# A new order for every engine's steps and a new layout of the PSUM banks in a four-layer graph network kernel

## The chip, the cores and the metric

The kernel runs on one core of one Trainium2 chip, in one launch. The metric is the device time in microseconds (us) of that core; lower is better. The core has TensorE (matrix products and transposes, into PSUM), VectorE, ScalarE and GpSimd, and SyncE, which here only issues transfers. In the profile's rows they are PE (PEld for its weight loads), DVE, ACT, POOL and SP. TensorE has a granted clock that the profile shows as a share of full speed: 1.00 is 2.4 GHz, 0.50 is 1.2 GHz.

## What is computed

The input x is 32 graphs of 512 nodes with 128 features in float32; one 512 x 512 adjacency matrix is shared by all. Four layers follow each other. Each adds to x what it computes from h = max(layernorm(x), 0):

```
layer 0: hW = h @ Wo; scores from two projections of hW, leaky 0.1, masked by adj, softmax over axis 1
         out = att @ hW + h @ Ws
layer 1: h1 = h @ Wp + bp; scores s_src + s_dst, leaky 0.2, masked, softmax, times adj, @ h1
         h_gat = relu(layernorm(...)); h_gin = (1 + eps) * h_gat + adj @ h_gat
         z = relu(layernorm(h_gin @ W1 + b1)); out = relu(z @ W2 + b2 + h_gat)
layer 2: Wh = h @ W; scores f1 + f2, leaky 0.2, masked, softmax, @ Wh, + bias, elu
layer 3: out = (A * I) @ (h @ W[0]) + (A * (1 - I)) @ (h @ W[1]) + bias
         A = softmax of edge weights that are placed by the rank of each edge in adj
x = x + out, after each layer
```

## The kernel before

**Tiling.** The 32 graphs are cut into 16 groups of two (G = 2). A group's x is one SBUF tile of 128 partitions by 1024 float32, eight blocks of 128 features. Six groups can be under way at a time (NS = 6 sets of buffers). Each group passes through 56 named steps (the list STEPS): for each the list gives the number of PSUM banks that it opens and the engines that take part. There is a 17th stream of nine steps (PREP, written as group 16 here, letter g in the strings), which makes layer 3's matrix A; layer 3 of the first groups waits for it.

**Order.** Nothing is scheduled at run time. Each engine walks a fixed list of (group, step) pairs, and waits on semaphores in its steps. The list is written as one string per engine, TURNS: the k-th letter is the group whose next step (of those in which this engine takes part) comes k-th. Steps of one group keep their order on an engine; only how the groups interleave is free. TensorE has 469 such steps, VectorE 471, ScalarE 403, GpSimd 160, SyncE 32 (loads and stores).

**Banks.** PSUM has eight banks of 128 x 512 float32. A second string, HOMES, has one digit for each bank that TensorE's steps open, in TensorE's order: the bank's number. A step that opens a bank waits until the last reader of what was in it before has freed it.

The lines that do this:

```
for e, turns in TURNS.items():
    todo = [(name for name, _, engines in steps if e in engines.split()) for steps in [STEPS] * GROUPS + [PREP]]
    order[e] = [(int(g, GROUPS + 1), next(todo[int(g, GROUPS + 1)])) for g in turns]
...
for g, name in order["pe"]:
    for n in range(tiles_of[name]):
        bank = int(next(home))
...
def open_tile(u, name, s, n=0):
    slot, k = u.tile(name, n)
    pe.wait_ge(taken[slot], k + 1)
```

**The steps that matter below.**
- *Normalisation* (four times per group, and gats1 and mlps1 in layer 1): stat0 to stat3, gats1, mlps1 are eight bn_stats on VectorE (line 1176) and then, on GpSimd, ten small steps on 128 x 8 tiles (lines 431 to 446, function rstd_of); then scale0 to scale3, gat1, mlpb1 are eight activations on ScalarE (line 450), and norm0 to norm3, mlpb1 are eight transposes on TensorE (line 704), which ScalarE copies to HT.
- *Layer 0*: coef0 (TensorE, line 687, wcols; VectorE, lines 1188 to 1196), cmax0 (TensorE, line 795; VectorE, lines 1201 to 1210; ScalarE exponentials, lines 969 and 970), coefp0 (GpSimd, four small steps, lines 1114 to 1117), coefb0 (TensorE, CS and adj_top; VectorE, lines 1222 to 1231), feat0 (TensorE, Wo), split0 (VectorE, lines 1237 and 1242, each twice; ScalarE copies HI and HIB, lines 975 and 982), low0 (VectorE LOW, line 1247; GpSimd LOWB, line 1122), agg0 (TensorE, maskT with HI and LOW), self0 (TensorE, with HIB, LOWB and Ws; VectorE adds).
- *Layer 1*: feat1, top1, weigh1, spread1, att1a and att1b (attention of the two graphs), collect1, gats1, gat1, gatl1, gin1, mlpa1, mlps1, mlpb1, mlpc1. *Layer 2*: feat2, sums2, top2, spread2, att2a, att2b, elu2a, elu2b, elu2. *Layer 3*: shift3, feat3, agg3.
- *PREP*: erow, eoffm, eedge, eat, ecover, evalue, emask, esoft (VectorE, lines 1431 to 1438, after ScalarE's exponentials) and eturn (TensorE transposes, line 893; ScalarE copies a_hi, line 1060; VectorE a_lo, line 1446).

The setup ahead of the ordered walk (loads, masks, weights) ends at about 24 us and is the same in both kernels.

Of the kernel before, what the change touches and what calls it, by code (L numbers as in the profile page):

```python
# [117 lines left out]
    ("eturn", 4, "pe act dve"),  # L118
]
TURNS = {  # L120
    "pe": ("gggg01011200201g100221313240030410041013314041252513132052025521243143232013031535040003100110104511"
           "4254251145540250245102132322124264262673667437762426373234343447333644768486465876858676738787535778"
           "348584588489559859659956a99a5a6a679a997969669569657a67a56767778a778a7b7b8a6b869baba6a78ab7b88978a8ba"
           "8cb8b8bbcd9bd9bdca8a8ccd9d899a9c9aa9ca9aa9edeadceacbcdeccbecdcd9edebd9b9edebedbeecbfcfbefbebffbbfcfd"
           "adafcfdfaffdcfcccfccedcddedcfdfededfbfdeeeebfeeffefeffbfcdfcdcedfefef"),
    "dve": ("g021gggg1010g02g001314010012113220503401401231340232210351034351221054524125433423001153500250012130"
            "0441105025145111452204303541262431252724626226676337644267376253743438334777464638436868857847687887"
            "3455637884984856579a895599956899a95a76655a99a996768a965a77a956a667b766787797abab86877aab6bbab7bbac89"
            "a788d8bab88bc88bd99cdba8accddc89b9c9aeca9adacd9aedd9eb9cac9cceedbedcedee9bb9dcecfeadeebacbfdfbbfffbb"
            "edfffbbdacfcfeffddccaefcccdfdfeccdfdeecdffdeedbefedfeeffbfefecffdcdefef"),  # L130
    "act": ("g02101g210g01334200410130240115053012102104150223113510322014323004100031125115442025502410325140521"
            "342135342226436472764346227233457343344468683667548758636775353868747545848796895587596a968a8665a979"
            "6996756a9566975797776a78a789b6b88667aba877b8aa79aa98bc8ab8ac9bd8bd9ba8ba8c8d9b9caa999adaaebecc9debdc"
            "c9cbecaddb9b9ceebdcbedefcbfcdbbeaeffcdcbdadfafdefdfccebfccfdcdefdfdecfefedffeebdefbefefffceddcfcdeef"
            "fef"),
    "pool": ("02110031402135420231350415420150310210214563274626237463784783586384547959a8969a657a5967a7b686b87b7a"
             "bc89da889cbdacaed9cde99ebcebfdbafcafefdcbdcfedfbefcedfcdefef"),
    "sp": "345020611728394a5b6c7d8e9fabcdef",
}
HOMES = ("0123456710234567102345671203645024502714365027127504127502741361436150274674361530263704204372047620"  # L140
         "4376204371506265043715423603165427031370137013701654270541653421670615342706156364270153615142703516"
         "5165421703267053267054105410326570413261357045740261357042613570426135710457263103142603142640231657"
         "1657164023042571642571264307127152756430127645301452376017604523601745021367450215036274150451045316"
         "2712716271627160475316205476231054762310765410765414072653721401640146537201420653714065371425306710"
         "6710642537061706170610760176017642534523476347652347652031476576457645642073156204062407316540731652"
         "4073152640731526430742615305310745236216216074536530652106352106743542354210674267410351032674032516"
         "0734516073451620762076345135135143541207635412075634120637541206375413270654506132702761302024502761"
         "4376052145421542145214376052176432174360536050356217407374560213745602145376021453760241537602415")


def bcast(ap, n):
# [14 lines left out]
def gnn_kernel(nc, x, adj, Wo_d, Ws_d, att0_d, Wp_d, bp_d, asrc_d, adst_d, gatg_d, gatb_d, eps_d, W1_d, b1_d,  # L166
# [12 lines left out]
    with ctx:  # L179
# [62 lines left out]
        tile_at, mat_at, mat_of = {}, {}, []  # L242
        opened, home = [0] * BANKS, iter(HOMES)
        for g, name in order["pe"]:
# [1277 lines left out]
```

How the kernel before makes its waits and increments, by code:

```python
            @block.sync  # L455
            def _(sp):
                for t in range(T):
                    sp.dma_start(adj_raw[:, t, :], adj[t * P:(t + 1) * P, :]).then_inc(adj_loaded, 16)
                for s in range(NS // 2):
                    for b in range(G):
                        sp.dma_start(X[s][:, b::G, :],
                                     x.rearrange("b (t p) f -> b p t f", p=P)[s * G + b]).then_inc(x_loaded[s], 16)
                for dst, src in REST:
                    sp.dma_start(dst, src).then_inc(loaded["rest"], 16)
                for s in taken:
                    sp.sem_inc(s, 1)
                for s in sig["stored"]:
                    sp.sem_inc(s, 16)
                sp.wait_ge(loaded["rest"], 16 * len(REST))
# [1 line left out]
            @block.gpsimd  # L472
# [3 lines left out]
                nc.gpsimd.memset(work1[:], 1.0).then_inc(made["pool"], 1)  # L476
                nc.gpsimd.memset(minus_half[:], -0.5).then_inc(made["pool"], 1)
                nc.gpsimd.memset(ones_r[:].bitcast(F32), 1.0).then_inc(made["pool"], 1)
                for zeros in (pick, bias_p, bias_1, bias_2):
                    nc.gpsimd.memset(zeros[:].bitcast(F32), 0.0).then_inc(made["pool"], 1)
                pool.wait_ge(made["pool"], 9)
                nc.gpsimd.affine_select(out=ident[:], in_=ident[:], compare_op=ALU.not_equal, fill=1.0, base=0,
                                        pattern=[[-1, P]], channel_multiplier=1).then_inc(made["pool"], 1)
```

## Time and profile before

| | before |
|---|---|
| median of 3 runs | 1011.76 us (1009.36 to 1011.84) |
| profiled execution, its own time | 1009.46 us |
| its span, first to last instruction | 1007.7 us |
| busy: TensorE, VectorE, ScalarE, GpSimd | 943.0, 866.1, 632.5, 566.6 us |
| TensorE's granted clock, mean | 0.979 |
| a load of a group's x, issue to landing | 3.5 us (median) |

How to read it: an engine's busy time is the union of its instructions' times; a wait shows as idle time in front of an instruction, with what ended it. A half clock shows not as idle time but as longer instructions. A view by windows gives busy time and the granted clock for each stretch, and the timeline merges equal instructions that follow each other into one row (x8 is eight of them).

### The profile page before, as it was taken

How to read it: one execution, taken by the hardware profiler on the slowest of the kernel's cores; microseconds unless marked ns; L12 is line 12 of the kernel's file. 1: busy time of each engine (PE TensorE's matmuls, PEld its weight loads, DVE VectorE, ACT ScalarE, POOL GpSimd, SP SyncE). 2: the span in 40 equal slices, each digit the busy share in tenths (PEclk: the TensorE clock that was granted, in tenths of full speed). 3: DMA queues.
4: the chain of work that ended last, by engine and by line, in shares of the span. 5: the costliest groups of instructions: out<-in, count | busy, mean ns of one | idle time of the engine just before them, and what ended most of it. 6: DMA issues, size and time to landing. Idle time of an engine off the chain costs nothing. (4 is left out here: it accounts for less than half of the span.)

```text
span 1007.7 us, 21096 instructions
## 1 busy us (share of the span) xinstructions
PE 943.0 (94%) x7355; PEld 901.4 (89%) x7355; DVE 866.1 (86%) x2526; ACT 632.5 (63%) x1655; POOL 566.6 (56%) x1171
## 2 busy tenths in 40 slices
PE   5879999999999989999989999999999999997998
PEld 4779998998988989998989999899999998997897
DVE  6879898899979999978989987789989887887973
ACT  3435746875777755676675756777458676666751
POOL 3416356655477662763748645736646475556750
PEclk9978999999999999999999999999999999999999
DMA  5011000000011010011000101100100100000012
GB/s 136 1 36 28 2 1 1 2 1 1 2 43 42 2 44 1 1 43 43 2 1 2 43 2 43 43 1 13 32 1 2 42 2 1 17 7 2 1 43 63
DMA packets 38069, 19.97 MB, mean 20 GB/s; under 512 B 3142, under 2 KB 37452, under 8 KB 37964
## 3 DMA queue, kind: packets, MB, share of 16 engines
q1 hardware_dynamic: 36080, 18.42, 6.6%
q8 instruction: 59, 0.97, 0.4%
q10 hardware_dynamic: 1884, 0.21, 0.2%
q14 instruction: 46, 0.38, 0.1%
HBM read 10.23 MB, written 8.39 MB: 18 GB/s over the span
## 5 line engine op out<-in xcount | busy, mean ns | idle before, releaser
L450 ACT ACTIVATE Y<-X,SM 128x128 f32<-128x128 f32 x512 | 204.3, 489 | 70.8 <-POOL SM L446 70.6
L687 PE MATMUL ps<-HE,PT 128*128 128x129 f32 x2048 | 240.2, 276 | 2.7 <-ACT HE L999 1.7
L687 PEld LDWEIGHTS ps<-HE,PT 128*128 128x128 f32 x2048 | 233.5, 192 | 4.1 <-ACT HE L999 1.9
L1311 DVE SCALAR_TENSOR_TENSOR PT<-ps,CE,maskT 128x512 f32<-128x512 f32 x256 | 173.0, 741 | 13.3 <-PE ps L811 13.0
L442 POOL TENSOR_TENSOR SM<-SM,minus_half 128x8 f32<-128x8 f32 x96 | 162.9, 1696 | 7.6
L431 POOL TENSOR_TENSOR SM<-ST 128x8 f32<-128x8 f32 x96 | 29.7, 310 | 230.8 <-DVE ST L1176 230.8
L687 PE MATMUL ps<-W,HT 128*128 128x128 f32 (+1 forms) x768 | 125.9, 312 | 0.0
L687 PEld LDWEIGHTS ps<-W,HT 128*128 128x128 f32 x768 | 116.4, 194 | 8.8
L1176 DVE BATCH_NORM_STATS2 ST<-X 128x6 f32<-128x128 f32 x512 | 104.7, 277 | 2.6 <-DMA X<-in_x_dram 1.0
L704 PE MATMUL ps<-ident,Y 128*128 128x128 f32 x640 | 86.3, 282 | 13.2 <-ACT Y L450 11.0
L704 PEld LDWEIGHTS ps<-ident,Y 128*128 128x128 f32 x640 | 74.5, 146 | 16.8 <-ACT Y L450 14.1
L959 ACT ACTIVATE HT<-ps 128x512 f32<-128x512 f32 x96 | 51.9, 593 | 37.1 <-PE ps L704 36.6
L687 PE MATMUL ps<-HI,a_hi 128*128 128x256 f32 x256 | 73.2, 286 | 0.0
L687 PE MATMUL ps<-HI,a_lo 128*128 128x256 f32 x256 | 72.0, 281 | 0.0
L687 PE MATMUL ps<-LOW,a_hi 128*128 128x256 f32 x256 | 72.0, 281 | 0.0
L999 ACT ACTIVATE HE<-ps,HE 128x128 f32<-128x128 f32 x256 | 68.9, 381 | 0.0
L450 ACT ACTIVATE HE<-Y,SM 128x128 f32<-128x128 f32 x128 | 51.0, 488 | 17.6 <-POOL SM L446 17.5
L687 PE MATMUL ps<-gin_hi,LOW 128*128 128x512 f32 x128 | 57.8, 451 | 0.0
L1176 DVE BATCH_NORM_STATS2 ST<-Y 128x6 f32<-128x128 f32 x256 | 51.8, 274 | 5.0 <-ACT Y L1028 4.6
L450 ACT ACTIVATE Y<-Y,SM 128x128 f32<-128x128 f32 x128 | 50.9, 485 | 8.1 <-POOL SM L446 8.0
L1122 POOL TENSOR_TENSOR LOWB<-HE,HIB 128x1024 fp32r<-128x1024 f32 x16 | 36.2, 2260 | 26.0 <-ACT HIB L982 26.0
L687 PE MATMUL ps<-gin_hi,HI 128*128 128x512 f32 x128 | 50.4, 394 | 0.0
(260 smaller groups left out, 2355.5 us busy)
## 6 DMA issues: line engine op xcount, KB each, us to landing
X<-in_x_dram SPq DMA_DIRECT2D x32, 256.0 KB, 3.5
out_dram<-X SPq DMA_DIRECT2D x32, 256.0 KB, 2.8
adj_raw<-in_adj_dram SPq DMA_DIRECT2D x4, 256.0 KB, 3.8
W<-in_L_gnn_W_dram SPq DMA_DIRECT2D x2, 64.0 KB, 3.8
W<-in_L_gnn_W_dram SPq DMA_DIRECT2D x1, 128.0 KB, 3.5
bias<-in_L_gnn_bias_dram SPq DMA_DIRECT2D x2, 64.0 KB, 3.9
Wo<-L_gnn_others_weight_dram ACTq DMA_DIRECT2D x1, 64.0 KB, 3.2
feat1w<-in_L_gnn_Wp_dram ACTq DMA_DIRECT2D x1, 64.0 KB, 3.6
```

The lines of the kernel that those rows point to most:

```text
L431: TT(sm[:, S_DIF, :], st[:, :, 1], st[:, :, 4], ALU.subtract)
L442: link(TT(sm[:, S_RSTD, :], sm[:, S_VAR, :], minus_half[:], ALU.pow))
L450: a = nc.scalar.activation(dst[:, n, 0:F], src[:, n, 0:F], func, scale=SM[s][:, S_RSTD, n:n + 1], bias=SM[s][:, S_SHIFT, n:n + 1])
L687: return nc.tensor.matmul(o, w, m, start=start, stop=stop, skip_group_check=True)
L704: mm = T_(o[:, t * P:(t + 1) * P], Y[s][:, t * G + b, 0:F], ident[:])
L959: a = A(HT[s][:, b, :], o, ACT.Relu)
L999: a = A(HE[s][:, k, 0:F], o[:, 2 * P * b:2 * P * b + F], ACT.Identity, scale=HE[s][:, k, F:F + 1])
L1122: TT(LOB[s], VA[s], HIB[:].bitcast(F32), ALU.subtract).then_inc(sig["by_pool"][s], 1)
L1176: a = V.bn_stats(ST[s][:, n, :], src(n))
L1311: a = V.scalar_tensor_tensor(out=PT[r][:, j, :], in0=o, scalar=CE[s][:, c:c + 1], in1=maskT[:, j, :].bitcast(F32), op0=ALU.max, op1=ALU.mult)
```

## The change

Only the strings TURNS and HOMES are new: no instruction is added, removed or resized. The new strings come from the same kind of planning as the old ones, with three costs changed in the plan: an instruction of VectorE and one of GpSimd in SBUF exclude each other, TensorE runs at half its clock for part of the time, and the banks are laid out again for the new order. On TensorE 335 of 469 steps stand at another place, by 1.6 places on average and 15 at most; on VectorE 360 of 471, by 1.9 and 16; on ScalarE 303 of 403, by 1.8 and 21; on GpSimd 88 of 160, by 0.8 and 4; on SyncE 7 of 32, by 3 at most.

The diff, cut to the first line of each string:

```diff
 TURNS = {
-    "pe": ("gggg01011200201g100221313240030410041013314041252513132052025521243143232013031535040003100110104511"
+    "pe": ("gggg011012102g20010012231340430401001013301242541311352052021245315240302352313510304003100110105411"
...
-    "dve": ("g021gggg1010g02g001314010012113220503401401231340232210351034351221054524125433423001153500250012130"
+    "dve": ("g120gggg101g02g2000314110001211324503001240133023121020413354312152042415542453030523511305020013120"
...
-    "act": ("g02101g210g01334200410130240115053012102104150223113510322014323004100031125115442025502410325140521"
+    "act": ("g10210g12g002133404010102305110435010122101450223131050123324102034103010215115044223505021432451304"
...
-    "pool": ("02110031402135420231350415420150310210214563274626237463784783586384547959a8969a657a5967a7b686b87b7a"
+    "pool": ("1020102341015342032134051540215031002142156327462632746738437883548645979a965896a575a679a7b8b6768ba7"
...
-    "sp": "345020611728394a5b6c7d8e9fabcdef",
+    "sp": "043506121728394a5b6c7d8e9fabcdef",
 }
-HOMES = ("0123456710234567102345671203645024502714365027127504127502741361436150274674361530263704204372047620"
+HOMES = ("0123456701234567012347056123476123476312405763123140623140623571471406237537151406235710645706156154"
...
```

Read out for the two stretches of which more is said (group:step):

```
TensorE, from the first norm0
before 0:norm0 1:norm0 0:coef0 1:coef0 1:cmax0 2:norm0 0:cmax0 0:feat0 2:coef0 0:coefb0 1:feat0 16:eturn 1:coefb0
       0:agg0 0:self0 2:cmax0 2:feat0 1:agg0 3:norm0 1:self0 3:coef0 2:coefb0 4:norm0 0:norm1 0:feat1
after  0:norm0 1:norm0 1:coef0 0:coef0 1:cmax0 2:norm0 1:feat0 0:cmax0 2:coef0 16:eturn 2:cmax0 0:feat0 0:coefb0
       1:coefb0 0:agg0 0:self0 1:agg0 2:feat0 2:coefb0 3:norm0 1:self0 3:coef0 4:norm0 0:norm1 4:coef0 3:cmax0 0:feat1
VectorE
before 16:emask 1:coef0 0:coef0 1:cmax0 0:cmax0 16:esoft 0:coefb0 2:coef0 16:eturn 0:split0 0:low0 1:coefb0 3:stat0
       1:split0 4:stat0 0:agg0 1:low0 0:self0 0:stat1
after  16:emask 1:coef0 0:coef0 1:cmax0 16:esoft 0:cmax0 2:coef0 16:eturn 2:cmax0 0:coefb0 0:split0 0:low0 3:stat0
       1:coefb0 4:stat0 1:split0 1:low0 0:agg0 0:self0 0:stat1
ScalarE
before 16:eedge 0:scale0 2:scale0 1:scale0 0:norm0 1:norm0 16:esoft 2:norm0 1:cmax0 0:cmax0 16:eturn 0:split0 1:split0
after  16:eedge 1:scale0 0:scale0 2:scale0 1:norm0 0:norm0 16:esoft 1:cmax0 2:norm0 16:eturn 0:cmax0 0:split0 2:cmax0

TensorE, late
before 15:self0 13:gin1 10:norm3 13:mlpa1 10:feat3 15:norm1 12:mlpc1 15:feat1 13:mlpb1 15:top1 10:agg3 15:spread1a
       15:spread1b 13:mlpc1 12:norm2 15:att1a ... 14:mlpa1 13:top2 12:att2b 15:gin1 13:spread2a 15:mlpa1 14:mlpb1
       13:spread2b 14:mlpc1 13:att2a 15:mlpb1
after  15:self0 13:mlpa1 12:mlpc1 10:norm3 11:att2b 10:feat3 15:norm1 15:feat1 15:top1 10:agg3 15:spread1a 13:mlpb1
       12:norm2 15:spread1b 13:mlpc1 ... 14:mlpa1 12:att2a 13:feat2 13:sums2 12:att2b 15:gin1 13:top2 15:mlpa1
       14:mlpb1 13:spread2a 13:spread2b 14:mlpc1 13:att2a 11:norm3 15:mlpb1
VectorE
before 15:self0 15:stat1 11:elu2 11:stat3 13:mlps1 10:feat3 12:mlpc1 15:feat1 12:stat2 15:top1
after  15:self0 15:stat1 13:mlps1 12:mlpc1 12:stat2 11:elu2b 10:feat3 14:gat1 15:feat1 15:top1 11:elu2 11:stat3
```

## Rows read from the trace of the kernel before

**Rows 1.** The page's head: the span, and busy us of each engine.
```profile
span 1007.7 us, 21096 instructions
...
PE 943.0 (94%) x7355; PEld 901.4 (89%) x7355; DVE 866.1 (86%) x2526; ACT 632.5 (63%) x1655; POOL 566.6 (56%) x1171
```

**Rows 2.** Windows: stretch, length, busy of each engine, granted clock, DMA, GB/s.
```profile
24.00:50.00 26.00, 23.00 (x111) 18.88 (x111) 22.96 (x57) 12.57 (x30) 11.17 (x30) 0.89 0.00 1
50.00:112.00 62.00, 53.62 (x356) 52.61 (x357) 51.42 (x171) 31.11 (x78) 25.32 (x65) 0.78 0.10 26
112.00:838.00 726.00, 701.03 (x5671) 674.77 (x5671) 648.91 (x1885) 480.50 (x1262) 429.75 (x896) 1.00 0.06 16
838.00:946.00 108.00, 96.75 (x729) 89.84 (x728) 88.45 (x249) 71.74 (x192) 65.88 (x127) 0.98 0.02 6
```

**Rows 3.** TensorE's timeline, 48 to 100: start, length, what; in brackets idle before.
```profile
48.32 5.63 PE L687 MATMUL ps<-wcols,HT 128*128 128x4 f32 x32
...
66.54 2.16 PE L893 MATMUL ps<-ident,v 128*128 128x128 f32 x16
...
74.51 0.58 PE L687 MATMUL ps<-HI,maskT 128*128 128x256 f32 x1 [4.59 <-DVE LOW L1247]
...
84.15 1.95 PE L687 MATMUL ps<-Wo,HT 128*128 128x128 f32 x16
87.76 0.39 PE L687 MATMUL ps<-HI,maskT 128*128 128x256 f32 x1 [1.67 <-DVE LOW L1247]
...
98.21 3.39 PE L704 MATMUL ps<-ident,Y 128*128 128x128 f32 x16
```

**Rows 4.** VectorE's timeline, 57 to 77.
```profile
57.77 0.42 DVE L1201 TENSOR_REDUCE MX<-ps 128x2 f32<-128x256 f32 x1 [1.17 <-PE ps L795]
...
58.90 2.29 DVE L1432 TENSOR_TENSOR v<-work,rinv 128x2048 f32<-128x2048 f32 x1
...
68.06 2.48 DVE L1446 TENSOR_TENSOR a_lo<-ps,a_hi 128x512 fp32r<-128x512 f32 x4 [2.26 <-ACT a_hi L1060]
70.81 1.29 DVE L1237 TENSOR_TENSOR Y<-ps,SM 128x512 f32<-128x512 f32 x2 [0.27 <-DVE a_lo L1446]
...
74.57 2.16 DVE L1225 TENSOR_TENSOR SM<-SM,CE 128x8 f32<-128x8 f32 x1
```

**Rows 5.** ScalarE's timeline, eturn's copies.
```profile
67.43 2.06 ACT L1060 ACTIVATE a_hi<-ps 128x512 fp32r<-128x512 f32 x4 [8.30 <-PE ps L893]
```

**Rows 6.** TensorE's timeline, 837 to 921.
```profile
837.53 0.48 PE L687 MATMUL ps<-gin_hi,LOW 128*128 128x512 f32 x1
...
842.15 1.04 PE L704 MATMUL ps<-ident,Y 128*128 128x128 f32 x8
...
851.29 1.24 PE L704 MATMUL ps<-ident,Y 128*128 128x128 f32 x8 [2.30 <-ACT Y L450]
...
869.93 1.09 PE L704 MATMUL ps<-ident,Y 128*128 128x128 f32 x8 [1.48 <-ACT Y L450]
...
908.88 1.13 PE L704 MATMUL ps<-ident,Y 128*128 128x128 f32 x8 [1.60 <-ACT Y L450]
...
913.54 3.74 PE L687 MATMUL ps<-HE,PT 128*128 128x129 f32 x32
...
919.10 1.97 PE L704 MATMUL ps<-ident,Y 128*128 128x128 f32 x16 [1.82 <-ACT Y L450]
```

**Rows 7.** The chain of work that ended last, 840 to 851.
```profile
840.39 1.66 DVE ST L1176 x8
842.12 1.11 POOL SM L431
...
848.05 3.19 ACT Y L450 x8
```

**Rows 8.** Instructions of line 431 and, below, 1247: ns minimum, median, maximum.
```profile
L431 POOL TENSOR_TENSOR SM<-ST x96: 200/209/1257, 31.3 to 974.4; 128x8 f32<-128x8 f32 x96
...
L1247 DVE TENSOR_TENSOR LOW<-Y,HI x16: 1214/1226/2936, 73.2 to 827.0; 128x1024 fp32r<-128x1024 f32 x16
```

More of the change, by code:

```diff
@@ L120 @@
 TURNS = {
-    "pe": ("gggg01011200201g100221313240030410041013314041252513132052025521243143232013031535040003100110104511"
[L122 to L125, printed above, removed]
@@ L126 @@
-    "dve": ("g021gggg1010g02g001314010012113220503401401231340232210351034351221054524125433423001153500250012130"
[L127 to L130, printed above, removed]
@@ L131 @@
-    "act": ("g02101g210g01334200410130240115053012102104150223113510322014323004100031125115442025502410325140521"
-            "342135342226436472764346227233457343344468683667548758636775353868747545848796895587596a968a8665a979"
-            "6996756a9566975797776a78a789b6b88667aba877b8aa79aa98bc8ab8ac9bd8bd9ba8ba8c8d9b9caa999adaaebecc9debdc"
-            "c9cbecaddb9b9ceebdcbedefcbfcdbbeaeffcdcbdadfafdefdfccebfccfdcdefdfdecfefedffeebdefbefefffceddcfcdeef"
+    "pe": ("gggg011012102g20010012231340430401001013301242541311352052021245315240302352313510304003100110105411"
+           "4252514515404425023150213212242642622636764374626723773332433443434767586486488643687678753876534577"
+           "848785458985958965998659a59656a7a9799a96a6996769675a665a7577678a787a7b7ba9a8bb9a8ab6a6b7b768788b8a89"
+           "8ab8b8bdbc9cbadccadb89c8dd9989ca9caa9adad9a9eaecaecbceecdbccc9dededb9b9eddebedbbeebcfefbcffefbdbfcfd"
+           "cabafffafdcfdcfccfeccdecddcfdfeddedbffdeeeebfefefefecffcbfdfdcedfefef"),
@@ new lines @@
+    "dve": ("g120gggg101g02g2000314110001211324503001240133023121020413354312152042415542453030523511305020013120"
+            "0441050151244153131452200451642312527246226226663374676423763723343478354773367864846488867785443887"
+            "6355794867845865979a8799956895959566a8a559979aa696a67a79568aa657967b6778797aba77b6aa88bbb6abbb769a7a"
+            "8c8d8ab88b8b8899cdcbadabc8cddc989c9dcaaed9cda9adbeabe9ca9c9cecbeecddeee9bbd9cdecefdbbeaeafdfbdcffbfb"
+            "efffdccbaeffbbaffdcdcefccefcfcddcfdeecdffddeedbefefdeeffebefcfffdcdefef"),
@@ L135 @@
+    "act": ("g10210g12g002133404010102305110435010122101450223131050123324102034103010215115044223505021432451304"
+            "12521435226462437264347622532733437436444386856638747836757354568486745756988957895765a96866a8597a97"
+            "69965796a76658957977a678a978bb87aa98b6967baa6787a8ba8b98a8a9cdbb8dcaa89bcb89d8ca999adaaabeeccbd9becc"
+            "abd9cec9bddb9ceebcdbedebfbcfdbdfceefcadcdeafafdbcffdcbfceccfdedeffdecffdedffebedfebefecfffcecddfedfe"
             "fef"),
-    "pool": ("02110031402135420231350415420150310210214563274626237463784783586384547959a8969a657a5967a7b686b87b7a"
-             "bc89da889cbdacaed9cde99ebcebfdbafcafefdcbdcfedfbefcedfcdefef"),
@@ L138 @@
-    "sp": "345020611728394a5b6c7d8e9fabcdef",
-}
-HOMES = ("0123456710234567102345671203645024502714365027127504127502741361436150274674361530263704204372047620"
[L141 to L148, printed above, removed]
+    "pool": ("1020102341015342032134051540215031002142156327462632746738437883548645979a965896a575a679a7b8b6768ba7"
+             "b9c8da898cdacb9deacde9bec9ebfdbfcafaefdcbdfcedfbefcefcddeeff"),
@@ new lines @@
+    "sp": "043506121728394a5b6c7d8e9fabcdef",
+}
+HOMES = ("0123456701234567012347056123476123476312405763123140623140623571471406237537151406235710645706156154"
+         "6701546702315453167024351264351706453121523170643512067351206735473457345120670304516247530316247037"
+         "0537016254256703427056341634127056324170561372437243743052617430526174137426051357142601357134260101"
+         "5705173426052605173426051472361405407236105436136172053646456317204563172063451720637245106370670362"
+         "4751757475475471036214762035471547105632471056324710456324506716710167324562743015630152630715426542"
+         "6542630714526425642563071426035603423047156230472315604723156047234723471560152347234760125473012504"
+         "1256127356127356127304156415627340156273423015642701536415214536470217025364620453620174536320415763"
+         "2415763240716524352435071606706701240350246710243560271546302715463027154306427135042761350135042761"
+         "3507641325302532053207641520523054170562365232635417027176350426317501750174263501742631507426315")
```

## Prediction

> **What bounds the kernel now.** I read the page's header first. TensorE is busy 943.0 us of 1007.7, VectorE 866.1 [rows 1], and the two work on different groups at once, so the time is TensorE's dense work plus what it waits and what it loses to its half clock. The table by windows says where the loss lies [rows 2]. The reader is to subtract TensorE's busy time from each window's length: 3.0 us idle of the 26 from 24 to 50, 8.4 of 62 from 50 to 112, 25.0 of 726 from 112 to 838, and 11.3 of 108 from 838 to 946. The clock column adds the rest: 0.78 in the window from 50 to 112, where it stands at 1.2 GHz part of the time and at 2.4 otherwise, gives 62 x 0.22 = 13.6 us of missing full-clock time, and in the long middle it is 1.00. So the early stretch loses about 22 us in 62, the middle 25 in 726, the late stretch 11 in 108. The middle is 96.6% busy, and there the order has little left to give; early and late the loss per microsecond is many times that.
>
> Then the timelines of those two stretches, TensorE's [rows 3] for the idle gaps, VectorE's and ScalarE's [rows 4, 5] for what comes late. Two gaps stand out: 4.59 us before agg0 of group 0 at 74.51 and 1.67 before agg0 of group 1 at 87.76, both ended by VectorE's LOW of line 1247 [rows 3].
>
> **The change part by part.** No instruction is added, removed or resized, so the dense sums stay: each change of time is a wait that goes or comes, or clock. Setup, erow and the first DMAs are untouched (the loads of groups 0 to 2 are issued before the ordered walk, and the reordered stores and loads lie beside 5% DMA use in the middle [rows 2]); I cost SP's seven moved steps at nothing, and if that cover failed the price would be one late load of a group, 3.5 us by the landing time in the table above. The banks are taken from another string; along the stretch that I walk below I went tile by tile, and each bank that is opened had its last reader at least a step earlier, so they cost nothing there.
>
> *The first join (groups 0 and 1 of layer 0).* Before, VectorE ran coef0 of 1 and 0, cmax0 of 1, waited 1.17, did cmax0 of 0 from 57.77, then esoft from 58.7 to 63.7 (its big multiply is the row at 58.90), coefb0 of 0 and coef0 of 2, waited 2.26 for ScalarE's copies, did eturn in 2.48, split0 in two halves of 1.29, and low0 in 1.23 [rows 4, 8]. TensorE could start agg0 only then, at 74.51 [rows 3]. After, coef0 of 1 comes first on TensorE, so VectorE has done it when coef0 of 0 arrives near 54.0, the end of the row at 48.32 [rows 3], and esoft follows cmax0 of 1 with no wait: it starts near 55.7, 3.0 earlier, and ends at 60.7. Then cmax0 of 0 (1.0) and coef0 of 2 (0.9) bring VectorE to 62.6. TensorE's eturn takes 2.16 [rows 3] from 61.4; ScalarE copies behind it (2.06, [rows 5]), VectorE's part ends near 65.2, cmax0 of 2 at 66.2. coefb0 of 0 must wait for ScalarE's exponentials, now behind its eturn, for four GpSimd steps of 0.2 [rows 8] and for TensorE's own part, about 0.9: 66.4. Then 1.3 for coefb0 (its row of 2.16 less the 2 us by which that one was stretched, and six more of 0.2), 2 x 1.29 for split0 with ScalarE's copy beside its second half, and 1.23 for low0 [rows 4, 8]: 71.5. agg0 of 0 starts 3.0 us earlier. A gap of some 4 us stays before it, since only coefb0 of 1 now lies between, so the half clock behind it stays too.
>
> *The second join.* Before, coefb0 of 1 stretched by 2 us (line 1225 took 2.16 beside GpSimd's LOWB), 3:stat0, split0, 4:stat0 and agg0 of 0 stood ahead of low0 of 1, and TensorE waited 1.67 more [rows 3, 4]. After, behind 71.5 come stat0 of 3 and 4 (1.65 each, as in [rows 7]), coefb0 (1.3), split0 (2.5) and low0 (1.23), and agg0 of 0 only behind them: low0 of 1 is done near 80. TensorE, with agg0 and self0 of 0 mostly at half clock (74.51 to 83.9, so 9.5), comes there at 81.0 and finds it. What it then does until norm1 of 0 is what it did before from 87.76 to 100.0, the middle of the row at 98.21, 12.2 us, and feat0 of 2, 1.95 from 84.15 [rows 3]: norm1 of 0 starts near 95.1 in place of 100. The lead is 5. The bounds are 0 (a stretch of 2 us, as line 1225's, at each join and one hand-over) and -9 (a third of the 13.6 us of clock goes as well).
>
> *The late stretch.* Four waits of TensorE for a normalised row stand here: 2.30, 1.48, 1.60, 1.82 [rows 6]. The first is norm1 of group 15. Its chain is in [rows 7]: statistics 1.66 on VectorE, then from 842.12 to 848.05 ten steps on GpSimd, the first of 1.11 where such a step has a median of 0.21 [rows 8] (the third was the same), then 3.19 on ScalarE. VectorE was in elu2, which reads two SBUF tensors. After, what follows the statistics on VectorE is mlps1 of 13, again statistics, so those 1.9 us go. On TensorE a gin1 (837.53 to 842.15, 4.6) leaves the space between self0 and norm1 of 15, and an att2b (3.7) and an mlpc1 (about 2.3) enter it [rows 6], so that it holds 12.6 us of work in place of 11.4. The gap goes. norm2 of 12 (1.48) now follows mlpc1 of 12 by seven steps more, among them agg3 and feat1: it goes. mlpb1 of 14 (1.60): between mlpa1 and mlpb1 lie now two att and a gin1 with small steps, some 16 us, in place of one att and that gin1: it goes. mlpb1 of 15 (1.82) stays, with about 1 us more of cover, but TensorE comes to it earlier by the 1.6; it grows to about 3. Against that stands a new wait: VectorE has gat1 of 14 and feat3 of 10 ahead of feat1 of 15, and TensorE comes to top1 of 15 some 1 to 3 us early. Sum: -2.3 - 1.5 - 1.6 + 1.2 + 2 = -2.2, and about -2 for the clock, which reads 0.98 of 108 us in this window [rows 2]: -4. Bounds: +2 (two of the waits come back at other places) and -8 of the 11.3 idle.
>
> *The middle.* By the same method (the work between a step and the one that waits for its way through the other engines, against the length of that way) I counted all 23 such returns of the 16 groups. In the middle the shortfalls sum to 13.6 us before and 9.1 after, over the whole kernel to 36.6 and 36.8, early ones being larger after. A count of cover leaves out queues, so I take less than half of the 4.5: -2. The bounds are -12 (half of the 25.0 idle goes) and +12.
>
> *A rule weighed.* GpSimd's first small step has median 0.21 and maximum 1.26, VectorE's LOW 1.23 and 2.94 [rows 8], so one engine stops while the other is in SBUF, by at most 1.05 and 1.71 in these rows. The Trainium skill, SBUF — State Buffer, "SBUF: two separate sides", says the pair of ports is locked for a whole instruction, and only by VectorE's instructions with two SBUF inputs or in a two-port mode; by that rule statistics never stop GpSimd, the first late gap goes whole (-2.3), where cover alone gives -1.2. The trace agrees in the one place where I looked (line 431 at 842.12, beside elu2).
>
> The Trainium skill, TensorE: Matmul & The Clock Gate, "What you observe", says that the ramp's penalty is under 1% of a typical kernel's span and need not be fitted. By that, the 2 us of clock in the late term would be nothing and the sum would be -9. The trace differs: 13.6 us of 1007.7 in one window.
>
> **Sum.** -5 early, -2 in the middle, -4 late: -11 us. The profiled execution took 1009.46 us (span 1007.7, so 1.8 around it), 2.3 under the median of 1011.76. -11 from its own time is 998.5, and against the median 1000.8. I predict 1001.
>
> **The rivals.** A measurement of this kernel can tell some 0.3%, 3 us, from no change.
>
> *Slower.* One mechanism: new collisions of VectorE and GpSimd in the middle. Eighty-eight of GpSimd's 160 steps and 360 of VectorE's 471 change places, and each two-input step that falls on a normalisation chain stops GpSimd's next small step by up to 1.05 us [rows 8]. It decides from fourteen more such stops on chains that TensorE waits for: 14 x 1.05 = 14.7 eats the 11 and passes 3. With sixteen, 16.8, the time is 1000.8 + 16.8 = 1017.6. For it: VectorE is 89% busy in the middle [rows 2], so a stop there is hard to win back. Against: all waits of the middle together leave TensorE 25.0 us idle, and sixteen more stops would raise that by two thirds, with cover a little larger than before.
>
> *Nothing to tell.* The early lead is lost again in the middle because VectorE, not TensorE, sets the pace at 648.9 of 726 [rows 2], and the late waits only move to top1 of 15 and mlpb1 of 15. For it: the shortfalls of the whole kernel are equal, 36.6 and 36.8. Against: VectorE has its work done earlier by the same lead. Time: 1011.
>
> *Only early or only late.* One of the two holds: -4 or -5, 1007.
>
> *More.* The middle's idle is halved as well: -12 in place of -2, 990.8. For it: the waits there are of the same kinds as the late ones. Against: the count of cover shows only 4.5.
>
> **How the numbers follow.** Chances: the forecast (996 to 1005) 0.43; more 0.16; only one of the two 0.16; nothing to tell 0.12; slower 0.13. So faster by over 0.3% 0.74 (1007 lies 5 below the median and counts there), the same 0.13, slower 0.13. The predicted time is the likeliest one's, 1001, whose own range is 996 to 1005. The range for 8 in 10 goes down to 989, the case of more and 2 us of spread, and up to 1012, which takes in the unchanged case; the slower one and about 0.05 at the low end stay out.
>
> **What would show it.** Right, if TensorE starts agg0 of group 0 near 71.5 with some 4 us idle before it, agg0 of group 1 without a gap, and norm1 of group 0 near 95; if no gap of over 1 us stands before norm1 of 15 and norm2 of 12 and a new one before top1 of 15. The window from 112 to 838, moved by the lead, should be shorter by about 2. Wrong, if esoft on VectorE starts later than 57, or if the middle's idle of TensorE is outside 13 to 37 us; the last would most likely break the forecast, since it has the widest bounds and I walked none of it.

## The result, and the profile after

The changed kernel takes 973.68 us (median of 4 runs, 972.01 to 976.05), the kernel before 1011.8 on the same chip: ratio 0.9628, 95% interval 0.9601 to 0.9655, so 37 to 38 us faster. The forecast was 1001.0 with a range of 989 to 1012. The direction was right, the size was more than three times too small, and the time lies outside the range. The profiled execution took 974.11 us.

The page's head after. Its busy times answer to [rows 1]:

```profile
span 972.4 us, 21097 instructions
PE 929.8 (96%) x7355; PEld 893.6 (92%) x7355; DVE 849.6 (87%) x2526; ACT 632.0 (65%) x1655; POOL 552.0 (57%) x1171
```

The span is 35.3 us shorter. With the same instructions VectorE is busy 16.5 us less and GpSimd 14.6 less, ScalarE the same. An order alone can't take that much busy time off an engine unless some of it was standing still inside an instruction.

The windows after, answering to [rows 2]:

```profile
24.00:50.00 26.00, 22.23 (x109) 18.71 (x107) 24.21 (x57) 12.70 (x30) 10.53 (x30) 0.89 0.00 1
50.00:112.00 62.00, 54.75 (x426) 53.03 (x426) 53.05 (x189) 34.92 (x87) 25.65 (x68) 0.89 0.10 27
112.00:838.00 726.00, 719.35 (x5857) 697.69 (x5857) 655.52 (x1949) 503.14 (x1324) 436.75 (x937) 1.00 0.06 17
838.00:946.00 108.00, 99.71 (x757) 93.17 (x756) 91.85 (x250) 64.39 (x174) 67.69 (x116) 0.98 0.03 10
```

Look at the middle one. TensorE's idle time fell from 25.0 us to 6.65, and 5857 products ran in the 726 us in place of 5671. 186 more of 5857 is 3.2%, 23 us of 726. The early clock rose from 0.78 to 0.89. The late window hardly changed: 8.3 idle for 11.3.

Where the time came from can also be read at steps that both traces have. TensorE's timeline after, at the joins of layer 0 and at norm1 of group 0:

```profile
71.14 0.58 PE L687 MATMUL ps<-HI,maskT 128*128 128x256 f32 x1 [4.35 <-DVE LOW L1247]
...
80.17 0.39 PE L687 MATMUL ps<-HI,maskT 128*128 128x256 f32 x1 [0.91 <-DVE LOW L1247]
...
93.54 1.09 PE L704 MATMUL ps<-ident,Y 128*128 128x128 f32 x8 [0.32 <-ACT Y L450]
```

And the same timeline late: norm1 of 15, feat1 and top1 of 15, mlpb1 of 14, mlpc1 of 15, norm3 of 12:

```profile
816.41 1.04 PE L704 MATMUL ps<-ident,Y 128*128 128x128 f32 x8
818.23 0.36 PE L687 MATMUL ps<-bias_p,pick 128*128 128x260 f32 x1 [0.78 <-ACT HT L959]
...
821.25 0.43 PE L802 MATMUL ps<-ident,MX 128*128 128x128 f32 x2 [0.51 <-DVE MX L1285]
...
867.63 1.04 PE L704 MATMUL ps<-ident,Y 128*128 128x128 f32 x8
...
879.81 0.47 PE L687 MATMUL ps<-bias,pick 128*128 128x512 f32 x1 [1.15 <-ACT HT L955]
...
910.90 1.94 PE L704 MATMUL ps<-ident,Y 128*128 128x128 f32 x8 [2.66 <-ACT HE L999]
```

Take two steps as anchors. Norm1 of group 0 stood near 100.0 before [rows 3] and starts at 93.54 now: a lead of 6.4. Norm1 of 15 stood at 851.29 [rows 6] and is at 816.41: 34.9. At the end the lead is 35.3. So 6.4 us came early, 28.5 in the middle and 0.4 late. Steps have changed places, so I also compared the two traces at equal amounts of TensorE's work (each step at its typical duration, summed along either order): the lead is 5.8 at 95 us, 7.7 at 125 to 150, 10.6 at 255, 16.5 at 467, 24.7 at 577, 31.2 at 685, 34.7 at 840, 41.5 at 930 and 35.4 at the end. The times are those of the trace before. The middle's gain isn't one place: the lead grows all along, though fastest from 467 to 685, where 14.7 us come. Late, some 7 us are won and 6 lost again around 910.90 of the new trace, where a gap of 2.66 is followed by a half clock (1.94 us for the eight transposes that take 1.04 at 867.63).

Two sources after, answering to [rows 8], line 1247 first:

```profile
L1247 DVE TENSOR_TENSOR LOW<-Y,HI x16: 1215/1222/1516, 69.9 to 794.7; 128x1024 fp32r<-128x1024 f32 x16
L431 POOL TENSOR_TENSOR SM<-ST x96: 199/209/1287, 30.9 to 940.8; 128x8 f32<-128x8 f32 x96
```

LOW's maximum fell from 2936 ns to 1516. GpSimd's first small step still meets a stop of 1.1 us somewhere.

What such a stop looks like, from the kernel before. VectorE's timeline at 567, then GpSimd's:

```profile
567.34 0.55 DVE L1295 TENSOR_TENSOR CF<-DS,MX 128x8 f32<-128x8 f32 x1
567.81 2.55 DVE L1297 TENSOR_SCALAR CF<-DS,MX 128x4 f32<-128x4 f32 x2
570.28 1.21 DVE L1366 SCALAR_TENSOR_TENSOR HE<-HE,X 128x1024 f32<-128x1024 f32 x1
```
```profile
565.97 1.89 POOL L1129 TENSOR_TENSOR HT<-SR,norow 128x1024 f32<-128x1024 f32 x1 [1.58 <-ACT SR L1005]
567.94 2.39 POOL L1131 TENSOR_TENSOR HT<-HT,bias 128x1024 f32<-128x1024 f32 x1
570.30 1.26 POOL L431 TENSOR_TENSOR SM<-ST 128x8 f32<-128x8 f32 x1
```

Line 1295 ends when line 1129 has ended (567.86); the two steps of line 1297, 0.22 us each alone, take 2.55 us together, nearly all of it the second, and end with line 1131 (570.33). Then the roles change: line 431, 0.21 alone, takes 1.26 and ends with VectorE's line 1366 (571.49). The first kind is the one that the forecast did not price: a tiny step of VectorE behind a long one of GpSimd, with the whole of VectorE's queue behind it.

### The profile page after: what moved, and what is told of

The parts are those of the page before. It is cut to its first block and busy times, and to the rows that moved or that the text cites. A ratio compares the mean times of both kernels' runs of the same rounds, so it can differ in the third digit from the quotient of the medians.

```text
span 972.4 us, 21097 instructions
## 1 busy us (share of the span) xinstructions
PE 929.8 (96%) x7355; PEld 893.6 (92%) x7355; DVE 849.6 (87%) x2526; ACT 632.0 (65%) x1655; POOL 552.0 (57%) x1171
## 5 line engine op out<-in xcount | busy, mean ns | idle before, releaser
L431 POOL TENSOR_TENSOR SM<-ST 128x8 f32<-128x8 f32 x96 | 27.5, 287 | 196.6 <-DVE ST L1176 196.5
L1136 POOL TENSOR_TENSOR X<-X,bias 128x1024 f32<-128x1024 f32 x16 | 38.9, 2434 | 21.0 <-ACT Y L450 21.0
```

Of the source, the lines that this page charges most:

```text
L431: TT(sm[:, S_DIF, :], st[:, :, 1], st[:, :, 4], ALU.subtract)
L1136: TT(X[s][:], X[s][:], repeat(bias3[:], TG), ALU.add).then_inc(sig["by_pool"][s], 1)
```

## Experiments

Times are medians. The ratio and interval are to the kernel before, measured on the same chip beside each group (1010.29, 1010.0, 1010.41 and 1009.72 us).

| kernel | us | ratio | 95% |
|---|---|---|---|
| before_banks | 1009.1 | 0.999 | 0.9978 to 1.0002 |
| after_banks | 974.66 | 0.9643 | 0.9617 to 0.9669 |
| before_fills | 975.75 | 0.9656 | 0.9625 to 0.9687 |
| after_fills | 964.0 | 0.9538 | 0.9516 to 0.9561 |
| before_fills_long | 983.68 | 0.9748 | 0.972 to 0.9776 |
| after_fills_long | 972.08 | 0.9625 | 0.9605 to 0.9646 |
| before_small | 1001.77 | 0.9919 | 0.9897 to 0.9941 |
| before_large | 989.77 | 0.9799 | 0.9778 to 0.9819 |
| new_start | 1005.08 | 0.9945 | 0.993 to 0.996 |
| old_start | 980.22 | 0.9699 | 0.9684 to 0.9713 |
| new_half | 997.89 | 0.9873 | 0.9856 to 0.9889 |
| after_warm | 976.0 | 0.9661 | 0.9643 to 0.968 |
| new_start_fills | 979.38 | 0.9704 | 0.9682 to 0.9727 |
| old_start_fills | 975.94 | 0.9666 | 0.9652 to 0.9681 |
| new_late | 1009.09 | 0.9994 | 0.9977 to 1.0011 |

**The banks.** The same orders, with HOMES laid out by one rule for both: each tile takes the bank that the trace shows freed first.

```diff
-HOMES = ("0123456710234567102345671203645024502714...")
+HOMES = ("0123456701234567012345670213456125612705...")   # before_banks
-HOMES = ("0123456701234567012347056123476123476312...")
+HOMES = ("0123456701234567012347056123476123476312...")   # after_banks, other from the 84th digit on
```

> The order of before, with the banks laid out anew by one plain rule: each tile takes the bank whose last reader ended first in the trace of before. If banks carry a large part of the gain, 1000 or less; if they carry nothing, within 4 us of 1011.8.

> The order of after, banks by the same plain rule from the trace of after. If the gain needs its own layout of the banks, above 985; if the order carries it, within 4 us of 973.7.

Measured: 1009.1 and 974.66, each within noise of its own order with its own banks. The layout of the banks is worth nothing that can be told in either order. The gain is the order of the steps.

**Stops taken away.** GpSimd's instructions that read SBUF become memsets of about the same length (called fills here), with the same waits and hand-overs. Left out of the output are the real row statistics, the low parts and biases that GpSimd would have made; all else runs as it did.

```diff
-            TT(sm[:, S_DIF, :], st[:, :, 1], st[:, :, 4], ALU.subtract)
-            ...
-            link(TS(sm[:, S_RSTD, :], sm[:, S_RSTD, :], 2.0, None, ALU.mult))
-            return TT(sm[:, S_SHIFT, :], sm[:, S_RSTD, :], sm[:, S_MEAN, :], ALU.mult)
+            fill(link, 104, 7 if not inv else 10)
+            fill(link, 512, 3)                  # 4 in the long version
+            link(nc.gpsimd.memset(sm[:, S_RSTD, :], 1.0))
+            return nc.gpsimd.memset(sm[:, S_SHIFT, :], 0.0)
-                    TT(LOB[s], VA[s], HIB[:].bitcast(F32), ALU.subtract).then_inc(sig["by_pool"][s], 1)
+                    fill(link, 512, 2)
+                    nc.gpsimd.memset(LOB[s].bitcast(F32), 0.0).then_inc(sig["by_pool"][s], 1)
```

and the same for coefp0, the mean and bias of layer 2 and the bias of layer 3 (lines 1114 to 1136).

> The order and banks of before; every GpSimd instruction of the ordered walk is replaced by memsets of about the same total length that read no SBUF (so the normalisation is left out: scale 1, shift 0, and LOWB, the mean row and the bias are constants). Two theories for the 38 us. Exclusion: the old order loses its time to VectorE and GpSimd stopping each other; then without these stops it falls to 975 to 985, and VectorE's busy time falls from 866 towards 835. Interleaving: the old order is worse by where PE's steps and banks stand, and stops matter little; then it stays at 1000 or above.

> The same replacement in the new order. Exclusion: it falls little, from 974 to 963 to 970, so that the two orders differ by 12 us or less. Interleaving: the two orders still differ by 25 us or more.

Measured: 975.75 and 964.0. The old order gains 34.5 us, the new one about 10; of a difference of 37 us 11.8 are left. But the row statistics on GpSimd had become shorter by the way, and this helps either order. So the pair was made again with one more fill in each chain:

> As before_fills, but GpSimd's way through a normalisation is 0.6 us longer, as long as the real one (there it was 3.4 us in place of 4.0). If the fall to 976 came from the shorter way and not from the missing stops, this is back near 1000; if it came from the stops, 985 or less.

> The same longer fills in the new order. Exclusion: 974 less the few stops that are left, 965 to 973, within 15 us of before_fills_long. Interleaving: 25 us or more under before_fills_long.

The lengths named here, 3.4 for 4.0 us, leave out the two memsets that close each chain. GpSimd's timeline shows the first and last rows of the first chain in the kernel before, in before_fills and in before_fills_long:

```profile
31.25 0.21 POOL L431 TENSOR_TENSOR SM<-ST 128x8 f32<-128x8 f32 x1 [11.78 <-DVE ST L1176]
...
35.08 0.20 POOL L446 TENSOR_TENSOR SM<-SM 128x8 f32<-128x8 f32 x1
```
```profile
31.39 3.39 POOL L431 MEMSET scr<- 128x104 f32 x10 [12.00 <-DVE ST L1173]
...
35.00 0.10 POOL L440 MEMSET SM<- 128x8 f32 x1
```
```profile
31.81 3.98 POOL L431 MEMSET scr<- 128x104 f32 x11 [12.24 <-DVE ST L1173]
...
36.01 0.10 POOL L440 MEMSET SM<- 128x8 f32 x1
```

That is 4.0 us for the real chain, 3.7 for the short one and 4.3 for the long one: the two pairs lie on either side of the real length. Measured with the long ones: 983.68 and 972.08. The old order gains 26.3 us, the new one 1.6 (as a ratio it is 0.9625 against 0.9628, so nothing that can be told). Half way between the pairs, which is an estimate for the real length, the old order gains about 30 us and the new one about 5. The difference between the orders is 11.8 us with short chains and 11.6 with long ones. So some 25 us of the 37 are stops that the new order doesn't pay for, and this doesn't hang on the length of the chain. The memsets don't take every stop away: in before_fills_long 8.0 us of stretched time are left on VectorE (the sum of what lies above the shortest instance of the same step, where that is 0.1 us or more; 31.3 in the kernel before).

**Which stops.** Only the normalisation's small steps become fills (before_small), or only the other GpSimd steps: coefp0, LOWB, the mean and the two biases (before_large). The diffs are the two halves of the one above, with long fills in before_small; each leaves out its half of GpSimd's results.

> The order of before; only the ten-step and fourteen-step chains of the normalisations are fills without SBUF reads (the normalisation is left out; scale 0.05, shift 0); LOWB, the mean row, the bias and the coefficients are computed by GpSimd as in before. If the stops that cost are those of GpSimd's short steps on the normalisation chains, as my slower rival priced them, 985 or less; if they are the long GpSimd instructions that hold VectorE, near 1000.

> The counterpart: the normalisation chains are real, and the coefficients, LOWB, the mean row and the bias (instructions of up to 2.5 us) are fills (constants in their place). If long instructions that hold VectorE cost most, 990 or less; if the short steps do, 1000 or more.

Measured: 1001.77 and 989.77, so -8.2 us and -20.2 us. The 8.2 is too low for the small steps alone. before_small has the long chains, 0.3 us over the real length, and from the two pairs above that costs the old order about 4 us (half of 983.68 less 975.75); an estimate for the small steps is then 12. The two parts add to about 32, near the 30 for both at once. The page's head, engines' line, of before_small, before_large, before_fills_long and after_fills_long:

```profile
PE 947.5 (95%) x7355; PEld 906.2 (90%) x7355; DVE 869.4 (87%) x2526; ACT 633.1 (63%) x1655; POOL 534.0 (53%) x1475
```
```profile
PE 939.7 (95%) x7355; PEld 902.5 (91%) x7355; DVE 837.9 (85%) x2526; ACT 633.2 (64%) x1655; POOL 538.0 (54%) x1363
```
```profile
PE 936.4 (96%) x7355; PEld 899.2 (92%) x7355; DVE 839.3 (86%) x2526; ACT 632.5 (65%) x1655; POOL 508.1 (52%) x1667
```
```profile
PE 932.9 (96%) x7355; PEld 896.9 (92%) x7355; DVE 836.0 (86%) x2526; ACT 632.8 (65%) x1655; POOL 508.2 (52%) x1667
```

Read the DVE column against 866.1 [rows 1]. With the large steps gone VectorE is busy 28.2 us less; with the small ones gone it isn't less at all (869.4), since the long GpSimd steps still hold it and the memsets of the chains can hold some of its steps as well (it has 38.7 us of stretched time for 31.3); what is won there is the chain on GpSimd. In the new order VectorE still stood still for 13.6 us (849.6 less 836.0), but the time that the new order gains without stops is only some 5 us: half of the standing still is gone, and most of the rest lies where it costs no time.

The groups of lines 1247, 1297 and 1295 in the kernel before, and the same three in before_large (there lines 1255, 1305 and 1303); the last numbers are busy us, mean ns, and idle before:

```profile
L1247 DVE TENSOR_TENSOR LOW<-Y,HI 128x1024 fp32r<-128x1024 f32 x16 | 25.3, 1583 | 3.0 <-ACT HI L975 2.9
L1297 DVE TENSOR_SCALAR CF<-DS,MX 128x4 f32<-128x4 f32 x64 | 19.5, 348 | 0.0
...
L1295 DVE TENSOR_TENSOR CF<-DS,MX 128x8 f32<-128x8 f32 x32 | 9.7, 305 | 1.1
```
```profile
L1305 DVE TENSOR_SCALAR CF<-DS,MX 128x4 f32<-128x4 f32 x64 | 12.7, 263 | 0.0
L1303 DVE TENSOR_TENSOR CF<-DS,MX 128x8 f32<-128x8 f32 x32 | 5.4, 169 | 1.1
L1255 DVE TENSOR_TENSOR LOW<-Y,HI 128x1024 fp32r<-128x1024 f32 x16 | 19.5, 1219 | 2.8 <-ACT HI L980 2.7
```

These three lines alone give back 16.9 of the 28.2 us (5.8, 6.8 and 4.3).

The middle window of before_fills_long and of before_large, against 701.03 and x5671 [rows 2]:

```profile
112.00:838.00 726.00, 718.70 (x5838) 694.63 (x5838) 646.01 (x1946) 499.35 (x1312) 400.06 (x1326) 1.00 0.06 16
```
```profile
112.00:838.00 726.00, 712.83 (x5768) 689.23 (x5767) 637.77 (x1924) 491.80 (x1289) 420.31 (x1065) 1.00 0.06 16
```

With the old order and few stops, TensorE idles 7.3 us in the middle, about as little as in the new kernel.

**Parts of the order.** The steps of TensorE, VectorE, ScalarE and GpSimd that start before a cut follow one order, the rest the other: new_start is new for TensorE's first 41 steps, which take in the joins and norm1 of group 0, and then old; old_start is the reverse; new_half is new for TensorE's first 229 of 469 steps; new_late is new only from the 382nd on, at about 838 us. SyncE's list is the old one in new_start, new_half and new_late and the new one in old_start. Banks by the rule of before_banks.

```diff
-    "pe": ("gggg01011200201g100221313240...    # old throughout
+    "pe": ("gggg011012102g20010012...          # new_start: the new string up to the cut,
+                                               # then the old one without the letters already used
```

> Every engine walks the new order for the steps that start in the first 112 us of the trace of after, then the old order for the rest; banks by the plain rule. The forecast's early term alone: 1011.8 - 5 to - 8, so 1003 to 1007. If the early lead is lost again in the old middle, 1010 to 1012.

> The old order for the steps that start in the first 120 us of the trace of before, the new order for the rest; banks by the plain rule. If the parts add: 973.7 + 6 to 8, so 980 to 982. The exclusion theory says that most of the gain lies behind the start, so under 985.

Measured: 1005.08, 5.3 us less than before, and 980.22, 30.2 less than before and 6.5 over the new kernel. The two parts add: 5.3 and 30.2 make 35.5 of the 36.7 between 1010.41 and 973.7. The first windows of new_start:

```profile
24.00:50.00 26.00, 22.00 (x108) 18.28 (x109) 23.76 (x57) 12.59 (x30) 10.80 (x30) 0.92 0.00 1
50.00:112.00 62.00, 56.42 (x426) 54.94 (x426) 54.58 (x191) 34.80 (x87) 25.65 (x68) 0.87 0.10 27
```

The clock of 0.87 is close to the new kernel's 0.89 and the 426 products are the same; the start keeps its gain in front of the old middle.

> The new order up to 480 us of the trace of after, the old order from there; banks by the plain rule. If the gain grows evenly with the steps, as the two traces lie beside each other (a lead of 20 to 22 us there): 990 to 992. If it needs one place, near 975 or 1010.

Measured: 997.89, -12.5, which misses the 990 to 992 expected. The comparison at equal work, made for this run's trace, says where: its lead over the kernel before is 18.0 us at 500 us and 11.3 at 520, and stays near 11 from there to the end. Between them TensorE has one long wait that neither whole order has, before cmax0 of group 10:

```profile
490.00 0.69 PE L795 MATMUL ps<-ident,MX 128*128 128x128 f32 x2 [5.82 <-DVE MX L1196]
```

So the first half of the gain did come, and the join of the two orders lost 6.7 us of it again; in front of the join the parts add up.

> The kernel before up to about 838 us, and from there the new order on every engine. The forecast's late term was -4 us: about 1006. The comparison of the two traces showed a net of about -1: about 1009. If the late order only pays when it stands behind the new middle (because the steps that lie over the seam fit each other), it is 1010 or slower.

Measured: 1009.09 against 1009.72: nothing that can be told. At equal work this run's lead is 0.9 us at 840 us, 7.7 at 930 and 1.6 at 985: the late order wins some 7 us and loses 6 again, as it does in the new kernel. The wait of 910.90 is here too:

```profile
944.76 1.09 PE L704 MATMUL ps<-ident,Y 128*128 128x128 f32 x8 [2.65 <-ACT HE L999]
```

**Clock at the start.** 17 products that nobody reads fill the gap of TensorE before agg0 of group 0, in the bank that agg0 then opens.

```diff
+                    if u.group == 0:
+                        o, _ = open_tile(u, "agg0", s, 0)
+                        for _ in range(17):
+                            MM(o, maskT[:, 0, 0:P], maskT[:, 0, :], True, True)
```

> The new kernel with 17 products of 128 x 512 added ahead of agg0 of group 0, in the 4.35 us in which TensorE waits there; their result is overwritten. If the half clock behind that gap still costs, agg0 and self0 of group 0 shorten by 1.5 us and the time falls by 1 to 3 us; if VectorE sets the pace there, no change.

Measured: 976.0, where the new kernel has 973.7: no gain. TensorE's timeline shows why:

```profile
66.23 4.13 PE L687 MATMUL ps<-maskT 128*128 128x512 f32 x17
70.73 0.39 PE L687 MATMUL ps<-HI,maskT 128*128 128x256 f32 x1 [0.37 <-DVE LOW L1251]
...
80.14 0.39 PE L687 MATMUL ps<-HI,maskT 128*128 128x256 f32 x1 [2.24 <-DVE LOW L1251]
```

The first product of agg0 now takes 0.39 in place of 0.58, so the clock is full there; but agg0 of group 1 still starts at 80.14 (80.17 without the fill), behind a gap of 2.24 in place of 0.91. What sets this pace is a load. VectorE's timeline in after_warm, and in the new kernel, at stat0 of group 3:

```profile
71.98 1.64 DVE L1180 BATCH_NORM_STATS2 ST<-X 128x6 f32<-128x128 f32 x8 [1.31 <-DMA X<-in_x_dram]
```
```profile
71.95 1.64 DVE L1176 BATCH_NORM_STATS2 ST<-X 128x6 f32<-128x128 f32 x8 [0.87 <-DMA X<-in_x_dram]
```

LOW of group 0 was done 0.4 us sooner in after_warm, but VectorE then waits for group 3's x, and the LOW that agg0 of group 1 needs comes no sooner. The full clock only moved idle time here; what it would be worth without that load is not shown.

**What is left without stops.** The two splices at the start, again with long fills.

> The kernel before, with the new start (as new_start) and with GpSimd's steps as fills of the normal length (as before_fills_long, which took 983.68 us; the new order with these fills took 972.08). Output: the normalised rows, biases and low parts are left out of it. Theory A, the start's gain is one of cover, clock and joins, and has nothing to do with stops: it is worth here what it was worth in new_start, 5.3 us, so about 978.4 us, and 6 us are left for the interleaving of the rest. Theory B, the start's gain was itself made of stops (LOWB and coefb0 at the joins): here about 983, within 2 us of before_fills_long. Theory C, all that is left between the two orders lies in the start: 972.

> The kernel after, with the old start (as old_start) and with the same fills in place of GpSimd's steps. It is the other side of new_start_fills. Theory A: 972.1 + 5 to 6.5, so 977 to 979 us. Theory B: 972 to 974. Theory C: 983.

Measured: 979.38 and 975.94. Against before_fills_long (983.68) and after_fills_long (972.08) the start is worth 4.3 and 3.9 us, near the first theory for new_start_fills, between the first and the second for old_start_fills, and well off the third. So of the 11.6 us that the fills don't take away some 4 are the start, and some 7.5 lie behind it, in how the groups interleave.

## Why the forecast failed

*The early term, -5: right.* new_start measured -5.3, old_start lost 6.5, and the anchors of the traces give 6.4. The marks on the way held too. VectorE's esoft starts at 55.96 (forecast 55.7), agg0 of 0 at 71.14 (71.5) with 4.35 us idle before it (some 4), norm1 of 0 at 93.54 (95). One mark missed: agg0 of 1 still waits 0.91 us, forecast none. Here a term that I had put at nothing came due: SyncE's moved steps. The new list loads group 4 ahead of group 3, while VectorE needs group 3 first, and it waits 0.87 us for that load at 71.95. In new_start, with the old list of SyncE, VectorE doesn't wait there and agg0 of 1 has no gap; but norm1 of 0 comes at 93.67 all the same, so this wait cost the kernel nothing that can be told. (Two slips carry nothing: the DMA share of the middle reads 0.06 in [rows 2], not 5%, and the chances of the three faster cases add to 0.75, not 0.74.) The clock, which I left out of the value and put into the bound, rose from 0.78 to 0.89 in the window from 50 to 112; 62 x 0.11 is 6.8 us of clock, while the lead there is little more than the forecast 5. How much of the lead is the clock no run separates: the forecast number was met with a clock gain that it didn't count.

*The late term, -4: wrong.* It is 0 (new_late) and 0.4 behind the second anchor. Step by step much of it came: no gap before norm1 of 15 (816.41), a shorter one than feared before top1 of 15 (0.51), none before mlpb1 of 14 (867.63), and mlpb1 of 15 has none while mlpc1 of 15 waits 1.15. But TensorE then meets 2.66 us at 910.90 and 1.02 at 894.25, which the forecast had not walked to (0.96 at 887.71, before feat2 of 14, stood in the old order as well). I summed waits that go without walking on to where the next one would stand. The 2 us of clock in this term didn't come either: the window reads 0.98 before and after. The Trainium skill, TensorE: Matmul & The Clock Gate, has its sentence on the ramp's penalty in the section "What's actually happening" and not in the one that the prediction names; by it these 2 us were nothing, and so they turned out. Early, no run decides for or against it.

*The middle term, -2: this is the step that failed.* Its size was taken from the count of cover, and what stops already cost was not in it. It measured 28.5 us between the anchors, against a bound of -12. Two bases of it were wrong.

First, its lower bound of -12 was half of TensorE's 25.0 us of idle time. The idle time of the middle fell by 18.3. A wait was taken as something that halves at best, and nothing in the trace of before gave a reason for that bound. Over the whole span TensorE's idle time fell by 22.1 us (64.7 to 42.6) and its busy time by 13.2 (943.0 to 929.8) with the same products. The mean clock, 0.979 before and 0.986 after, accounts for about 7 of the 13.2. For the other 6 I have no row; they are open.

Second, stops were priced in one direction only. The forecast weighed 1.05 us for each stop of a small GpSimd step behind VectorE, and only as a danger of the new order. It read the other direction, LOW's maximum of 2.94 and line 1225's 2.16 [rows 4, 8], as two odd rows. They were samples of the main cost: VectorE's steps held by LOWB, the mean and the biases. Making those long GpSimd steps memsets gives 20.2 us, against some 8 to 12 for the small ones. The means of the old trace would have shown it: line 1247 is 1583 ns on average over a minimum of 1214, line 1297 348 over 215, line 1295 305 over 166. Summed over all of VectorE's steps, what lies above the shortest instance of the same step (0.1 us and more) is 31.3 us in the trace of before, in 24 instructions, and 15.4 in 13 after; for GpSimd 60.8 and 45.7. The first number stood in the old trace, and the runs bear it out: in before_fills_long VectorE is busy 26.8 us less, and 8.0 us of such stretches are left.

*The count of cover*, 13.6 against 9.1 in the middle, took less than half of 4.5. It counted work on TensorE against the length of each way, and took a held step of VectorE for a part of one way. In fact the steps behind it in VectorE's queue are late as well, for other groups. That the way of counting missed the cost is measured; that it is the queue that multiplies it is my reading of rows like that at 567.81.

*The rivals.* "Slower", by new collisions, was near the right mechanism with the wrong sign: the order has fewer, and those that counted most held VectorE and not GpSimd. "Nothing to tell" said that VectorE sets the pace of the middle. That VectorE matters is borne out: in before_large, where it is held least, TensorE's idle time in the middle falls to 13.2 us. But it was no floor at its old busy time, as 26.8 us of that were standing still. "More", at 990.8, was the nearest and still 17 us off. The mark for wrong that I had set, the middle's idle time outside 13 to 37 us, was hit with 6.65.

*What stays open.* The 7.5 us behind the start that the fills leave; the 6 us of TensorE's busy time; what the clock gave early; and how the 25 us spread over single stops. The fills show the sum, not the places.

## What to carry to other kernels

Before judging an order by idle time, take each engine's busy time apart: for each line compare mean with minimum, and sum what lies above it; a tiny step with a maximum ten times its minimum is a stop, and all that is queued behind it pays. Price stops in both directions, the long instruction's victims first: here the long GpSimd steps cost 20 us of 1010 and the short ones some 8 to 12. When a step is replaced to take it out of the account, measure the replacement's length in the trace, last step included, and bracket the real one. If two orders are joined, look for a wait at the join before reading the sum. And never take a share of the visible idle time as the most that an order can win; keep the whole of it, and the stretched time of the other engines, inside the range.

## What the runs showed of the hardware

A step of VectorE can be held for the whole of a GpSimd instruction, up to 2.4 us for one of 0.22. Which steps are held can be seen in before_fills_long, where GpSimd only writes. VectorE's timeline there (lines 1292, 1294 and 1170 are 1295, 1297 and 1173 of the kernel before), then GpSimd's:

```profile
224.27 1.19 DVE L1294 TENSOR_SCALAR CF<-DS,MX 128x4 f32<-128x4 f32 x2
224.54 0.94 DVE L1170 TENSOR_SCALAR SM<-Y 128x8 f32<-128x8 f32 x1
...
505.17 0.17 DVE L1292 TENSOR_TENSOR CF<-DS,MX 128x8 f32<-128x8 f32 x1
```
```profile
224.48 0.96 POOL L1127 MEMSET HT<- 128x1024 f32 x1
...
504.33 2.29 POOL L431 MEMSET scr<- 128x512 f32 x4
```

The TENSOR_SCALAR steps still end only with the memset (at 225.44 to 225.48). The TENSOR_TENSOR at 505.17 runs in its 0.17 us in the midst of one; all 32 of its line take 166 to 169 ns, and LOW never exceeds 1227 ns. In the kernel before, both kinds were held. The Trainium skill, SBUF — State Buffer, "SBUF: two separate sides", says that a VectorE instruction with two SBUF inputs takes the shared ports only against a GpSimd instruction that reads SBUF, and one in a two-port mode against any; these rows agree, if TENSOR_SCALAR on 128 x 4 and 128 x 8 float32 runs in such a mode here, which they suggest and nothing else in this case shows.

Such stops count as busy time and so stay out of sight: 26.8 us of VectorE's 866.1 go when GpSimd's steps become memsets, and GpSimd's own 566.6 fell to 552.0 by the order alone.
